# Four reorderings in one fused transformer layer: first projections into idle score banks, later weight casts, slot placement one shared block sooner, rows split sooner in the last blocks

## What is computed

```python
qkv = x @ Wqkv                       # (8, 512, 3 * 256)
q, k = rope(q), rope(k)
out = softmax(q @ k.T / 4) @ v       # 16 heads
x = layernorm(x + out @ Wo)
n = x * rsqrt(mean(x * x)) * norm_weight
shared = relu(n @ sw1 + sb1) @ sw2 + sb2          # 256 -> 1024 -> 256
probs = sigmoid(n @ router_w.T); top 2 of 8, weights normalised
routed = sum over the 2 of w * (relu(n @ ew1[e] + eb1[e]) @ ew2[e] + eb2[e])
return layernorm(x + shared + routed)
```

## Time and profile before

| what | value |
|---|---|
| median of 3 runs | 1311.24 us (1308.58 to 1312.24) |
| the profiled execution | 1311.47 us, of it 1309.6 us from the first to the last instruction |
| PE busy | 1221.8 us, 93% |
| ACT, DVE, POOL busy | 995.9, 976.1, 567.7 us |
| mean granted clock of PE | 0.968 of full |

### The profile page before, as it was taken

The page is one execution under the profiler, slowest core; times in us unless marked ns, Lnnn a source line. Parts: engine busy times, 40 slices in busy tenths (PEclk is TensorE's granted clock), DMA queues, the critical chain, the costliest instruction groups (busy, mean ns, idle before and its releaser), DMA issues.

```text
span 1309.6 us, 29563 instructions
## 1 busy us (share of the span) xinstructions
PE 1221.8 (93%) x9377; PEld 936.7 (72%) x9440; DVE 976.1 (75%) x1945; ACT 995.9 (76%) x2039; POOL 567.7 (43%) x574
## 2 busy tenths in 40 slices
PE   3799999999999999868999979999999999999896
PEld 2444444444444444337899969999999999999896
DVE  5788887888788888628666647877777777777578
ACT  4599998999899999846744437777787777777677
POOL 5332322232223220006446654666666666666553
PEclk8799999999999999988799989999999999999998
DMA  9300101010000000432013237777777777776354
GB/s 298 111 18 3 34 2 36 2 34 2 20 2 18 2 18 18 140 115 89 18 54 110 85 104 242 241 240 238 239 251 249 249 243 246 238 240 219 109 186 160
DMA packets 125412, 161.25 MB, mean 123 GB/s; under 512 B 17088, under 2 KB 108224, under 8 KB 125312
## 3 DMA queue, kind: packets, MB, share of 16 engines
q1 hardware_dynamic: 118496, 141.25, 33.2%
q0 software_dynamic: 6816, 18.75, 4.0%
HBM read 122.06 MB, written 37.52 MB: 122 GB/s over the span
## 4 chain that ended last, share of the span: by engine, by line
PE 77%; DMA 9%; DVE 6%; ACT 3%; issue 2%; POOL 2%; SPq 0%; ACTq 0%; another core or an unknown queue 0%; DVEq 0%; POOLq 0%
PE att_psV L387 9%; PE att_psA L330 9%; PE att_psB L340 8%; DMA slots_x<-sent_rows,all_slot 6%; PE exp_psU L1587 5%; PE exp_psU L1589 5%; PE exp_psU L1588 5%; PE exp_psD L1572 5%; PE exp_psD L1573 5%; PE exp_psD L1574 5%; PE att_psT L354 4%; PE att_psX L408 2%; PE att_psX L410 2%; PE att_psX L409 2%; PE exp_psT L1560 1%
## 5 line engine op out<-in xcount | busy, mean ns | idle before, releaser
L529 DVE TENSOR_REDUCE att_mx<-att_psA 128x1 f32<-128x512 f32 x512 | 338.0, 683 | 74.2 <-PE att_psA L330 73.2
L445 ACT ACTIVATE att_prob<-att_psB 128x512 f32<-128x512 f32 x512 | 299.2, 599 | 53.0 <-PE att_psB L340 39.3
L1632 ACT ACTIVATE exp_psU<-exp_psU,ew_b 128x256 f32<-128x256 f32 x312 | 126.9, 446 | 103.2 <-PE exp_psU L1589 103.2
L330 PE MATMUL att_psA<-att_qk 96*128 96x512 bf16 x512 | 196.7, 386 | 6.2 <-DVE att_mx L529 2.4
L340 PE MATMUL att_psB<-att_qk 128*128 128x512 bf16 x449 | 172.6, 386 | 14.1 <-issue 5.4
L1683 DVE CAST exp_hh<-exp_psU 128x512 fp32r<-128x512 f32 x156 | 107.9, 692 | 101.6 <-ACT exp_psU L1632 101.6
L1572 PE MATMUL exp_psD<-exp_w2h,exp_hh 128*128 128x256 f32 x624 | 175.8, 282 | 0.0
L1587 PE MATMUL exp_psU<-exp_xh,exp_w1h 128*128 128x256 f32 x624 | 173.6, 278 | 1.4 <-DVE exp_xl L1674 1.4
L1589 PE MATMUL exp_psU<-exp_xh,exp_w1l 128*128 128x256 f32 x624 | 173.2, 278 | 0.0
L1588 PE MATMUL exp_psU<-exp_xl,exp_w1h 128*128 128x256 f32 x624 | 173.2, 278 | 0.0
L1573 PE MATMUL exp_psD<-exp_w2l,exp_hh 128*128 128x256 f32 x624 | 172.5, 276 | 0.0
(11 more groups left out here) (206 smaller groups left out, 3228.7 us busy)
## 6 DMA issues: line engine op xcount, KB each, us to landing
ew_w<-ew SPq DMA_DIRECT2D x40, 1024.0 KB, 5.6
exp_w<-ew SPq DMA_DIRECT2D x38, 1024.0 KB, 5.8
slots_x<-pre_acc SPq DMA_DIRECT2D x13, 780.0 KB, 10.3
pre_spare<-slots_x SPq DMA_DIRECT2D x39, 260.0 KB, 4.6
out_g<-rows_y SPq DMA_DIRECT2D x32, 256.0 KB, 3.2
ew_b<-eb SPq DMA_DIRECT2D x39, 128.0 KB
pre_spare<-xT SPq DMA_DIRECT2D x8, 512.0 KB, 4.5
attn_rows<-att_ob SPq DMA_DIRECT2D x8, 512.0 KB, 2.8
```

Source lines behind the costliest of these rows:

```text
L330: pe.matmul(psA[A_BANK[n % U]][:, :], r[:, 0, qt * P:(qt + 1) * P], r[:, 1, :], start=True, stop=True).then_inc(s_amm, 1)
L445: act.activation(prob[:, n % PR, :], psB[B_BANK[n % U]][:, :], ACT.Exp, scale=SCALE).then_inc(s_exp, 1)
L529: dve.reduce_max(mx[:, g % 2, n % U:n % U + 1], psA[A_BANK[n % U]][:, :], AX_X).then_inc(s_max, 1)
```

## The change

Four edits, none of which adds or removes an instruction that computes.

- In attention the first four q/k tiles take `psX` and `psA[0]` in turn, and the first two v tiles take `psA[1]`, with a short list of waits of their own (`take_first`: a q/k tile waits until the tile two before it has been read, a v tile until the v tile before it has been copied). `rope` and `copy_v` read from the same banks.
- `SPLIT_FROM` goes from 6 to 10: casts in slots 10, 12, ... 24, where they were in 6, 8, ... 20.
- `RANK_AFTER` goes from 1 to 0, and `place()` stands ahead of the third `rows_lo` and the first `add` on DVE.
- In combine `hidden_lo` of block 0 goes from DVE to POOL; ACT splits the rows of block n+1 ahead of block n's first `relu`, where it did so after its fourth; DVE's `rows_lo` of block 2 stands after the second pair, where it stood after the first.

```diff
--- before.py
+++ after.py
@@ -76,6 +76,7 @@
     HEAD = FIRST
     QK_LEAD, V_LEAD = 6, 4
     FILL = NT
+    ASIDE_QK, ASIDE_V = (1, 3), (0, 1)
     T_LEAD = A_LEAD + 5
     PIECES = 3
 
@@ -357,6 +358,13 @@
 
             QK, OUT, MAX, VALUE = range(4)
 
+            def take_first(tile, value):
+
+                if value:
+                    wait(pe, None, s_vev, tile, 1)
+                else:
+                    wait(pe, None, s_qrd, tile - 1, 1)
+
             def take_psX(p, use, it):
 
                 if it is not None:
@@ -398,11 +406,19 @@
             def project(tile, c, it, value):
                 b, t = tile // NT, tile % NT
                 if c == 0:
-                    take_psX(tile - (V_LEAD if value else QK_LEAD), VALUE if value else QK, it)
+                    if it is None and (tile in ASIDE_V if value else tile < FILL):
+                        take_first(tile, value)
+                    else:
+                        take_psX(tile - (V_LEAD if value else QK_LEAD), VALUE if value else QK, it)
                     if t == 0 and not value:
 
                         pe.wait_ge(s_xl, b + 1 if it is None else b + 1 + it * 2)
-                o, cols = (psX[:, 0:D], slice(2 * D, 3 * D)) if value else (psX[:, :], slice(0, 2 * D))
+                bank = psX
+                if it is None and value and tile in ASIDE_V:
+                    bank = psA[1]
+                if it is None and not value and tile in ASIDE_QK:
+                    bank = psA[0]
+                o, cols = (bank[:, 0:D], slice(2 * D, 3 * D)) if value else (bank[:, :], slice(0, 2 * D))
 
                 rows = slice(t * P, (t + 1) * P)
                 pe.matmul(o, xh[:, b % 2, c, rows], wh[:, c, cols], start=(c == 0), stop=False)
@@ -462,7 +478,8 @@
                 wait(act, it, s_vmm, tile + 1, 1)
                 if t == 0:
                     wait(act, it, s_pv, NT * HG * (b - 1), NT)
-                act.activation(V[:, b % 2, t, :, 0:DH], psX[:, 0:D].rearrange("p (h d) -> p h d", d=DH), ACT.Copy).then_inc(s_vev, 1)
+                bank = psA[1] if it is None and tile in ASIDE_V else psX
+                act.activation(V[:, b % 2, t, :, 0:DH], bank[:, 0:D].rearrange("p (h d) -> p h d", d=DH), ACT.Copy).then_inc(s_vev, 1)
 
             def spread(tile, it):
                 b, t = tile // NT, tile % NT
@@ -573,7 +590,7 @@
 
             def rope(tile, k, it):
                 b, t = tile // NT, tile % NT
-                x, half = heads_of(psX), DH // 2
+                x, half = heads_of(psA[0] if it is None and tile in ASIDE_QK else psX), DH // 2
 
                 def table(tb, c0, c1):
                     return tb[:, t, c0:c1].unsqueeze(1).to_broadcast([P, 2 * H, c1 - c0])
@@ -706,7 +723,7 @@
     NB = T // (NT * P)
     TILES = NB * NT
     SWP = DC * sw1.shape[1] // 512
-    SPLIT_FROM = 6
+    SPLIT_FROM = 10
     QT, RING = 4, 8
     assert TILES % QT == 0
 
@@ -1086,7 +1103,7 @@
 
     TILES, E = m.logits.shape[1], m.logits.shape[2]
     NB = m.early_blocks
-    RANK_AFTER = 1
+    RANK_AFTER = 0
     POOLED = 2
     LOOPED = (NB - 1) // 2 * 2
     BIASED = TILES // 4
@@ -1276,9 +1293,9 @@
             shared.rows_lo(dve, Nth(0))
             choose()
             shared.rows_lo(dve, Nth(1))
+            place()
             shared.rows_lo(dve, Nth(2))
             shared.add(dve, Nth(0))
-            place()
             with dve.Fori(1, LOOPED // 2) as it:
                 for k in range(2):
                     do(Nth(k, it))
@@ -1763,9 +1780,7 @@
 
         @block.gpsimd
         def _(pool):
-            for n in range(1, NB):
-                if n == 1:
-                    pool.wait_ge(shared.lo_ready, shared.HC)
+            for n in range(NB):
                 for h in range(shared.HC):
                     shared.hidden_lo(pool, Nth(n), h)
 
@@ -1807,15 +1822,13 @@
 
             pr.after_last(dve)
             shared.rows_lo(dve, Nth(0))
-            for h in range(shared.HC):
-                shared.hidden_lo(dve, Nth(0), h)
             rows_ahead(1)
             for k in range(PAIRS):
                 n = ORDER[k] - EARLY
                 if n >= 0:
                     shared.add(dve, Nth(n))
                 add_up(k)
-                if k == 0:
+                if k == 1:
                     rows_ahead(2)
                 if n >= 0:
                     rows_ahead(n + 3)
@@ -1854,11 +1867,11 @@
             shared.rows_hi(act, Nth(0))
             for slot in range(NORM[-1] + 1):
                 n, h = divmod(2 * slot, shared.HC)
+                if h == 0 and n + 1 < NB:
+                    shared.rows_hi(act, Nth(n + 1))
                 if slot < SLOTS:
                     shared.relu(act, Nth(n), h)
                     shared.relu(act, Nth(n), h + 1)
-                if h == 2 and n + 1 < NB:
-                    shared.rows_hi(act, Nth(n + 1))
                 for k in range(PAIRS):
                     if ROOT[k] == slot:
                         root(k)
```

## The result

The changed kernel takes **1293.9 us** in the median (1293.46 to 1294.97, 4 runs) against 1311.73; the ratio is 0.9873 (95% interval 0.9859 to 0.9888). That is 17.8 us less, where 20.5 were forecast and 1291 given, inside the range. The profiled execution has a span of 1292.4 us, 17.2 less than before.

The account below looks back on a forecast made before the run. PE, busy 93% of the span, was taken as the bound, with four holes where it stands. Gains of 6.8 + 2.8 + 6.5 + 4.4 = 20.5 us from 1311.24 gave 1291, with a range of 1286.5 to 1296.5 for 8 in 10.

Parts of the forecast that it names:

- edit 3: Shared blocks: slots one block sooner start the scatters 7.8 us sooner, blocks then end last; 6.5 us gained, bounds 3.5 and 7.
- edit 2: Norm stage: later casts remove ACT's 7.07 us wait for the weights; 2.8 us gained, bounds 0 and 4.
- Two of the signs that the prediction named for itself being wrong: Prediction wrong if first rows still wait for a scatter, or attention behind its first head grows.
- Edit 1: Attention's start: POOL becomes the pace at 3.63 us a tile, first head at 31.2; 6.8 us gained, bounds 3.6 and 7.2.
- What follows is as before: Attention behind the first head: unchanged, as maxima are needed some 17 us later and the zeros' DMA traffic is over.
- so it waits for them until about 593.1 ... 3.6 us sooner: Norm stage: DVE waits for residual rows until about 593.1, having reached tile 8 at 596.67 before; 3.6 us sooner.
- 0.3 to 0.9; I take 0.8: Norm stage: cost in us of up to three more POOL remainders falling behind tile 8 and slowing DVE.
- edit 4: Last stage: PE's 2.63 us gap and the half clock behind it go; 4.4 us gained, bounds 2.6 and 4.8.
- the scatters still end last: Rival, shared stage: scatters outlast the blocks despite a forecast 1.3 us margin the other way; time 1294, chance 0.12.
- End of the blocks 775.1: Shared stage: blocks end last at 775.1, first rows loaded then instead of at 781.66; 6.5 us.
- PE lost 0.7 us there: Shared block 2: DVE's remainders stood behind the placement, costing PE 0.7 us, which goes.
- The rule weighed there: Shared stage: two-input DVE and SBUF-reading GpSimd instructions shut each other out; the sum loses at most 0.3 us.

Follow-up runs that it names:

- e5: The changed kernel run again with no edit: median 1291.8 us, ratio 0.9863 to the kernel before.
- e2: The kernel before with only the later casts (first cast in slot 10 instead of 6): ratio 1.004, on a slower chip.
- e4: The kernel before with only the combine (last stage) edit: ratio 0.999, on a slower chip.
- e10: e9 with one wait added on PE ahead of down of block 1, until the placement is through: median 1286.95 us, ratio 0.9829.
- e12: e10 with the first cast in slot 12 instead of 10: median 1333.0 us where the kernel before took 1348.8, ratio 0.987.
- e6: The changed kernel with the weight loads moved behind the residual rows of tiles 8 to 11: 1289.7 us, ratio 0.9833.
- e11: e9 with the casts back in slots 6, 8, ..., rows still asked for ahead of the weights: median 1296.0 us, ratio 0.9883.
- e9: The same program as e6, run once more: 1290.0 us, ratio 0.9846 to the kernel before.
- e7: The changed kernel with the two counting matmuls behind down of block 0 instead of ahead of it: median 1294.8 us, ratio 0.9881.
- e1: The kernel before with only the spare banks for the first attention projections: ratio 1.001, on a slower chip.
- e3: The kernel before with only the count after block 0 and the placement moved earlier: ratio 0.999, on a slower chip.
- e8: The changed kernel without the earlier count and placement: median 1299.3 us (2 runs), ratio 0.991.

## Why the prediction was right or wrong

**The total** was right in direction and inside the range; the gain was 17.8 us for 20.5. It is partly right by luck: two terms of edit 3 were wrong with opposite signs, and edit 2 gave its gain in the first execution and not in the four others. Two of the signs that the prediction named for itself being wrong did come, attention behind its first head grew by 1.6 us in the first pair, and in e5 the first rows waited for a scatter. The parts below say what each was worth.

**Edit 1: right, in mechanism and size.** POOL's pace of 3.63 was read from rows 3, the fifth projection began at 28.29 for 28.3, the last spread at 29.40 for 29.35, and the head came at 31.21 for 31.2. Nine other executions with the edit had it at 31.12 to 31.32.

**"What follows is as before": off by 1.6 us in the first pair, cause open.** Attention behind the head lasted 535.6 to 539.7 us in four executions without the edit (mean 537.0) and 536.2 to 538.4 in ten with it (mean 537.4). A difference of 0.4 can't be told from that scatter. Most of it arises at one place: PE begins to turn the twelfth group of heads 18.8 us after the eleventh in the kernel before, 20.3 in the changed one, 18.7, 21.8 and 20.2 in e2 to e4 without the edit, and 18.5 and 18.6 in e10 and e12 with it. That edit 1 costs attention a little is neither shown nor excluded.

**Edit 2: the number was right and the step wrong.** The step that failed is "so it waits for them until about 593.1 ... 3.6 us sooner". The wait was there, and in the first execution the gain was 3.0. But I priced one landing time of a DMA as fixed, and what follows the wait at "0.3 to 0.9; I take 0.8". Five executions with the edit and the weights ahead of the rows had tile 8 at 18.7 to 20.9 us after attention and a norm stage of 72.2, 74.2, 75.4, 75.8 and 75.0; four without it had tile 8 at 22.1 to 22.6 and a stage of 75.2, 74.5, 74.3 and 74.4. The means of the stage are 74.5 and 74.6, so these nine show no gain of the edit alone, though the five spread by 3.6. Cut at tile 8, the two wrong terms come apart. Tile 8 came 2.5 us sooner in the mean, where 3.6 was said. From tile 8 to the stage's end it took 52.2 to 52.5 us without the edit and 53.5, 55.0, 54.9, 54.9 and 55.4 with it: 1.0 more in the first execution, 2.5 to 3 more in the others, where 0.8 was said. In those four PE was at half clock for 6.8 us behind its wait at tile 8, in the first for 3.4. In the kernel before the same 6.8 us of half clock lay almost all ahead of tile 8, in the catching up behind ACT's wait. e12, with as many remainders behind tile 8 and the full clock, took 52.3, so the clock rather than the remainders costs the rest. I named that cost for edit 4 and not here. e6, e10 and e12 show the other half of the remedy: the rows asked for first and the casts late give 71.1, 69.4 and 68.6, late casts being needed too (e11). e9, with 74.8, shows that slot 10 is then not always late enough.

**Edit 3: the mechanism was right, one term mis-sized twice.** All that was said of the order came true: slots ahead of POOL, POOL the last to be ready, 64 scatters in some 100 us, scatters and blocks through within 4 us of each other. Of the rival "the scatters still end last" both sides occurred: blocks last in the first execution, scatters last in e5, which was nevertheless the better one (125.3). The term that failed is "End of the blocks 775.1", the old length of the blocks carried over. PE's pace was taken as a constant of the kernel and is not: it was 0.1133 in the shared stage of the traced execution of before and 0.1178 in that of after, about 20 half blocks of 0.21 us = 4.2 us. (Both paces stood in the trace of before: its last stage ran at the 0.118 that the prediction reads there.) The same term was wrong the other way too: "PE lost 0.7 us there" counts one of five stops. Timeline of PE in the kernel before, `down` of block 2 to `up` of block 3:

```profile
681.08 0.36 PE L1070 MATMUL shr_psD<-all_sw_hi,shr_hh 128*128 128x256 f32 x1 [0.66 <-DVE shr_hl L1055]
...
682.65 0.39 PE L1070 MATMUL shr_psD<-all_sw_hi,shr_hh 128*128 128x256 f32 x1
...
683.65 0.39 PE L1070 MATMUL shr_psD<-all_sw_hi,shr_hh 128*128 128x256 f32 x1
...
684.65 0.39 PE L1070 MATMUL shr_psD<-all_sw_hi,shr_hh 128*128 128x256 f32 x1
...
687.84 0.28 PE L1030 MATMUL shr_psU<-shr_xh,all_sw_hi 128*128 128x256 f32 x1
```

DVE, late from the placement, made the remainders of two hidden rows a us, and PE followed it: this `down` began 0.8 late and took 6.8 us instead of 5.44, 2.1 in all. The edit took all of it away; with it the blocks' last addition stands at 123.5 to 124.0 at the faster pace (e5, e9, e10, e11), where 125.3 was forecast. So at the faster pace the edit gives 132.5 - 125.3 = 7.2, with the scatters last, and at the slower one 3.8, with the blocks last; forecast 6.5. The first scatter was also 1.8 us later than said: POOL's remainders began 0.7 later and took 0.2 longer, and the three copies with the wait behind them took 1.8 where I had 0.9. It cost nothing at the slower pace; at the faster one, where the scatters end last by about 1 us, up to that.
The rule weighed there (the Trainium skill, SBUF — State Buffer, "Who interferes with whom") lets a DVE instruction with two SBUF inputs and a POOL instruction that reads SBUF hold each other up. In the first execution only the last 1.7 us of the way to the slots lay beside POOL, and it cost POOL 0.2 (6.08 for its eight remainders against 5.85) and the slots 0.2. In e7 they overlapped for the whole 5.84, and the trace agrees with the rule on DVE's side: the scans with two SBUF inputs went from 0.22 to 0.70 us, a reduction with one input stayed at 0.29, and the slots came 3.5 us later. POOL lost nothing there, so all of the cost fell on DVE.

**Edit 4: right, in mechanism and size.** 4.6 for 4.4 in the first pair, both at a pace of 0.1178, and 4.6 in e4 against e1 to e3, all at 0.1133. The experts' stage, not touched, varies by 2 us (452.3 to 454.5), of which the first pair had 0.6.

## What to carry to other kernels

A wait that is taken away is worth what the next one leaves, and the next one must be priced with its spread and with what it does to PE's clock; one execution's landing time of a DMA is a draw. When two loads and two users wait in a row, both ends may have to move: late casts alone gave a stage of 74.5 in the mean, the rows asked for first with the casts early 77.8, and both together 68.6 to 74.8. And when two traces of one kernel differ by a few per cent in a stretch where PE never waits, compare the distance of its matmuls before looking for a cause in the edit.

## What the runs showed of the hardware

- **Two paces of PE at full clock.** A stream of 128x128 weights and 256 columns each ran at 0.1133 us a matmul (starts 0.11, 0.11, 0.12 apart) or at 0.1178 (0.12, 0.12, 0.12, 0.11), the same program at either. A stretch starts in one when the clock rises and keeps it; a short stop can change it. In the first three shared blocks that happened from 0.1178 to 0.1133 in six executions (e12 behind 0.26 us, e11 behind 0.45, e1, e2 and e4 behind less than 0.25, e8 behind the short waits of block 2) and from 0.1133 to 0.1178 in one (e3, behind a stop of 0.57 us at the count). As many stops changed nothing: those of e5, e7, e9 and e10 at 0.1133, the count in the changed kernel and in e6 at 0.1178. What in PE holds the pace, and which stop moves it, is open.
- **A two-input DVE instruction beside POOL.** A scan of 128x32 with both inputs in SBUF took 0.22 us alone and 0.67 to 0.70 beside POOL's subtractions of 128x256, which stayed at 0.73 (e7).
- **Chips.** On two chips PE, ACT and DVE all stood now and then in the looped shared blocks while POOL scattered, ACT for up to 19.90 us in e12 where it idles for 5.2 in each block of e5, and no longer once the scatters were over. The other stages were as long as elsewhere. The cause is open; no run takes the scatters or the loop away.

Timeline of ACT in e12, in the middle of the scatters:

```profile
748.90 0.47 ACT L1057 ACTIVATE shr_h<-shr_psU,all_sb 128x256 f32<-128x256 f32 x1 [19.90 <-remote]
```
